# Two transformer layers on one core: the opening's stores reordered, preparation spread over more turns, first queries before the barrier, and the last batch's output in two halves

## The chip, the cores and the metric

One core of a Trainium2 chip. The metric is the device time of one execution in microseconds (us), as the median of several. The core's engines are PE (TensorE), DVE (VectorE), ACT (ScalarE), POOL (GpSimd) and SP (SyncE, which only issues DMAs here). Each runs its own queue of instructions in order, and they meet through semaphores. All matrix products and transposes write into PSUM. The kernel cuts it into three slots of 128 x 1024 float32 (`slot[0..2]`) that are used in turn (`RING = 3`), and `yspace`, two banks of 512 columns.

## The reference, cut to what matters

```python
x = L0_attn_x                                  # (4, 1024, 128) float32
xn = layernorm(x)
x = x + attn0(xn) + ffn0(xn)                   # 16 heads of 64, causal, keys and values from a latent of 128
                                               # ffn0: silu-gated, hidden 352, inputs and weights rounded to FP4 in blocks of 16
xn = layernorm(x)
x = x + attn1(xn) + ffn1(xn)                   # 16 heads of 8, bias by relative position, biases on q, k, v, out
return x                                       # ffn1: 512 wide, ternary weights, gelu
```

## The kernel before

It has three blocks, each with a barrier of all engines at its end (each engine drains its own work first).

**Block A, the opening.** SP and ACT issue the loads. The DVE takes mean and variance of each of the 32 tiles of 128 tokens (`first_moments(b)`, 8 tiles of a batch: 8 `bn_stats`, 8 `bn_aggr`), normalises batch 0 and rounds it to FP4 (`fp4`, ten steps, `fp4_steps` L1807), then rounds the two FFN weights. ACT takes the square roots (L353, L397). PE transposes by `groups`; ACT copies the results out of PSUM in the order of that list. The position biases of layer 1 are split in bfloat16 parts: `x_part` (parts 0, 1, 2, each the rest of the one before; DVE L310, L329; ACT L360). SP stores them to DRAM at L229 and L231 after `off_act` 8, and then sixteen rows-of-steps (`step_rows`, L236) after `steps_set` 4.

**Block B, layer 0.** 32 turns, one for each batch (4) and pair of heads (8). In a turn PE computes the scores of the pair (L745, in four passes of high and low halves of queries and keys), DVE takes row maxima (L1006, L1009), ACT the exponentials (L930), PE transposes the probabilities (L780) and multiplies by the values (L792). One tile of the FFN goes along (gates, `hidden`, `down`). At the end of a turn PE computes the next turn's queries (`next_queries`, L695), ACT copies them rounded (L892, the high half), and DVE subtracts to get the low half (L972), which frees the slot; meanwhile PE runs `down` (L832) and `project` (L841). DVE adds their results to `x_tok` (L1076, L1084). The first score tile of the next turn goes into the slot of the queries.

Batches 1 to 3 are prepared on the way, half a batch at a time (`PREPS = 6`, `PREP_TURNS = 2, 6, 10, 14, 18, 22`, counted from 0): DVE does eleven steps (`prep_ops`: normalise, L628, then the ten of `fp4_steps`) in the two turns before, at two places of each turn (`prep(it, 0)` ahead of L1076, `prep(it, 1)` behind L1084), cut as 1, 4, 3 and 3 steps. In the preparing turn PE transposes (L803) and makes the latent (L810), and ACT copies (L958). From turn 8 on, DVE also takes the layer 1 statistics of one finished tile in each turn (`moments_of`).

**Block D, layer 1.** Its opening projects queries, keys and values of each batch (list `CT`; L1417, L1425), with the FFN woven in (`up` L1434, `down` L1443), DVE normalising (L1716) and taking low halves (L1723). Then 16 quads (4 batches, 4 groups of four heads): per quad 32 tasks `x` (scores with bias, L1566 and L1572; exponential on ACT, L1661), 16 `attend` (L1538) and, except in the last quad, 32 tasks `m` for the maxima of the next quad (L1458, L1463; DVE L1678). `AV_BEFORE` and `M_BEFORE` are a hand-written order of these. The output of a batch is normalised in halves `c` of 512 tokens (`normalise`, L1769, L1771), gathered (`y_gather`, eight transposes, L1490), copied by ACT (`copy_yT`, L1652), projected (`project`, L1497), added (`add_out`, L1779) and stored. For the first three batches this lies inside the next quad (`YT_AT = 8`, `OUT_AT = 13`); for the last batch it comes after everything else (L1592 to L1595, store L1361).

## Time and profile before

| | |
|---|---|
| time, median of 3 runs | 2309.61 us (2309.35 to 2309.88) |
| the profiled execution's own time | 2304.86 us |
| its span, first to last instruction | 2303.1 us, granted TensorE clock 0.993 |
| block A (opening) | 0 to 50.8 us |
| block B (layer 0) | 50.8 to 1372.1 us |
| block D (layer 1) | 1372.1 us to the end; the quads from 1480.7 |
| busy | PE 2154.1 us (94%), PE weight loads 1347.6, DVE 1670.4 (73%), ACT 1319.2 (57%), POOL 47.5 |

A row of a timeline gives the start and the duration in us, the engine, the line of the kernel, the operation, what it writes and reads, how many instructions are merged (x), and in brackets how long the engine was idle before it and what released it. A `q` behind the engine's name is its instruction queue, which issues the DMAs.

### The profile page before, as it was taken

The page shows a single profiled execution, that of the slowest core. Times are in us where ns is not written, and L with a number is a line of the kernel's source. Part 1 is how long each engine was busy: PE and PEld are TensorE (multiplying, and loading weights), DVE is VectorE, ACT ScalarE, POOL GpSimd, SP SyncE. Part 2 cuts the span into 40 slices and gives each one's busy share as a digit, 9 for nine tenths or more (in the row PEclk, how much of TensorE's full clock was granted, in tenths as well). Part 3 has the DMA queues.
Part 4 walks back from the last instruction along what each step waited for, and adds up shares of the span by engine and source line. Part 5 has one row for each costly group of instructions (what it writes and reads, how often), then busy time and mean ns, then how long its engine had stood idle before and what let it go on. Part 6 is the DMA issues. An engine that isn't in the chain of part 4 may idle for free. (4 is left out here: it accounts for less than half of the span.)

```text
span 2303.1 us, 45467 instructions
## 1 busy us (share of the span) xinstructions
PE 2154.1 (94%) x19387; PEld 1347.6 (59%) x19387; DVE 1670.4 (73%) x2208; ACT 1319.2 (57%) x2121; POOL 47.5 (2%) x61
## 2 busy tenths in 40 slices
PE   3999999999999999999999999999999999999998
PEld 1666767666666676667667666544444444444443
DVE  6786777777777767777777775777777777777771
ACT  2655655546555465555655553366666666666666
POOL 3100000000000000000000000200000000000000
PEclk7999999999999999999999999999999999999999
DMA  5000000000000000000000019311011011111000
GB/s 121 1 1 1 1 1 1 1 1 1 1 1 1 1 1 1 1 1 1 1 1 1 1 20 223 69 20 20 20 20 29 23 29 33 23 20 20 11 2 11
DMA packets 41195, 42.60 MB, mean 18 GB/s; under 512 B 21345, under 2 KB 33601, under 8 KB 40866
## 3 DMA queue, kind: packets, MB, share of 16 engines
q1 hardware_dynamic: 39842, 39.05, 8.1%
q8 instruction: 154, 2.52, 0.5%
q10 hardware_dynamic: 1152, 0.64, 0.1%
q14 instruction: 47, 0.39, 0.1%
HBM read 27.71 MB, written 11.70 MB: 17 GB/s over the span
## 5 line engine op out<-in xcount | busy, mean ns | idle before, releaser
L1678 DVE TENSOR_REDUCE nm_half<-slot 128x2 f32<-128x1024 f32 x512 | 606.5, 1222 | 162.8 <-PE slot L1463 118.0
L1661 ACT ACTIVATE pT<-slot 128x1024 f32<-128x1024 f32 x512 | 505.8, 1026 | 269.0 <-PE slot L1572 214.5
L930 ACT ACTIVATE prob<-slot,negmax 128x1024 f32<-128x1024 f32 (+6 forms) x448 | 316.8, 718 | 265.3 <-DVE negmax L1009 192.0
L745 PE MATMUL slot<-k_hl,q_hl 64*128 64x512 f32 (+3 forms) x2560 | 355.8, 359 | 66.6 <-ACT prob L930 60.2
L745 PEld LDWEIGHTS slot<-k_hl,q_hl 64*128 64x128 f32 x2560 | 261.4, 186 | 106.6 <-ACT prob L930 79.8
L780 PEld LDWEIGHTS slot<-ident,prob 128*128 128x128 f32 x2304 | 254.1, 141 | 88.7 <-issue 61.4
L780 PE MATMUL slot<-ident,prob 128*128 128x128 f32 x2304 | 288.7, 275 | 0.9 <-DVE probT L609 0.9
L609 DVE COPY probT<-slot 128x768 f32<-128x768 f32 (+1 forms) x192 | 166.7, 868 | 152.0 <-PE slot L780 149.1
L792 PE MATMUL yspace<-probT,v_sb 128*64 128x512 f32 (+3 forms) x1536 | 276.2, 494 | 0.0
L1538 PE MATMUL yspace<-pT,v 128*32 128x512 f32 x2048 | 267.0, 604 | 1.6 <-ACT y_raw L1648 0.8
L1566 PE MATMUL slot<-qs,ks 49*128 49x512 f32 x1024 | 240.2, 471 | 15.1 <-DVE nm_half L1678 7.5
L911 ACT ACTIVATE probT<-slot 128x1024 f32<-128x1024 f32 x192 | 170.1, 886 | 146.4 <-PE slot L780 123.7
L1458 PE MATMUL slot<-ks,qs 48*128 48x512 f32 x1024 | 241.4, 471 | 11.0 <-DVE nm_half L1678 8.3
L1009 DVE TENSOR_REDUCE negmax<-slot 128x1 f32<-128x1024 f32 (+2 forms) x192 | 191.5, 1039 | 71.6 <-PE slot L768 71.6
L1458 PEld LDWEIGHTS slot<-ks,qs 48*128 48x128 f32 x1024 | 95.9, 184 | 152.7 <-DVE nm_half L1678 85.8
L1566 PEld LDWEIGHTS slot<-qs,ks 49*128 49x128 f32 x1024 | 95.5, 185 | 133.6 <-DVE nm_half L1678 59.3
L792 PEld LDWEIGHTS yspace<-probT,v_sb 128*64 128x64 f32 x1536 | 96.5, 136 | 113.0 <-issue 90.6
L1572 PE MATMUL slot<-band,flipb 64*128 64x176 bf16 (+4 forms) x3456 | 161.3, 226 | 0.0
L1572 PEld LDWEIGHTS slot<-band,flipb 64*128 64x128 bf16 x3456 | 106.2, 95 | 49.4 <-issue 36.4
L745 PE MATMUL yspace<-k_hl,q_hl 64*128 64x512 f32 (+2 forms) x512 | 110.4, 355 | 0.0
L1006 DVE TENSOR_REDUCE negmax<-slot 128x2 f32<-128x1024 f32 (+3 forms) x128 | 97.0, 800 | 0.0
L930 ACT ACTIVATION_READ_ACCUMULATOR prob<-slot,negmax 128x1 f32 x448 | 90.3, 202 | 0.0
(236 smaller groups left out, 2326.9 us busy)
## 6 DMA issues: line engine op xcount, KB each, us to landing
qs<-q_hi SPq DMA_DIRECT2D x64, 64.0 KB
qs<-q_lo SPq DMA_DIRECT2D x64, 64.0 KB
ks<-k_hi SPq DMA_DIRECT2D x64, 64.0 KB
ks<-k_lo SPq DMA_DIRECT2D x64, 64.0 KB
x_tok<-in_L_attn_x_dram SPq DMA_DIRECT2D x4, 512.0 KB, 7.0
q_hi<-qk_out SPq DMA_DIRECT2D x4, 512.0 KB, 4.1
q_lo<-qk_out SPq DMA_DIRECT2D x4, 512.0 KB, 5.7
k_hi<-qk_out SPq DMA_DIRECT2D x4, 512.0 KB, 6.0
```

Source lines behind the costliest of these rows:

```text
L745: nc.tensor.matmul(own_ps[a][:, o:o + m], q_hl[hq][own, i * P:(i + 1) * P], k_hl[hk][own, o:o + m], start=(k == 0), stop=(k == 3 and o + m ...
L780: last = nc.tensor.transpose(ps[:, a * BANK + j * P:a * BANK + (j + 1) * P], prob[a][:, p_at(4 * c + j, kt)], ident[:, :])
L792: last = nc.tensor.matmul(ybank[c][a * HS:(a + 1) * HS, j0:BANK], v_sb[:, kt, a * HS:(a + 1) * HS], probT[m % PT_BUFS][:, a, j0:BANK], sta ...
L911: copy_probT(act, it, m, lambda out, src: nc.scalar.activation(out, src, ACT.Copy))
L930: last = nc.scalar.activation(prob[a][:, p_at(i, 0, w)], ps[:, o:o + w], ACT.Exp, bias=negmax[:, i, a:a + 1], accum_out=sums[:, i, a:a + 1])
L1009: nc.vector.tensor_reduce(negmax[:, i, a:a + 1], ps[:, 0:w], AX.X, ALU.max, negate=True).then_inc(neg_ready, 1)
L1458: last_ = nc.tensor.matmul(ps[:, a * BANK:(a + 1) * BANK], qs[s][own, p, i * P:(i + 1) * P], ks[s][own, p, h * BANK:(h + 1) * BANK], start ...
L1538: last_ = nc.tensor.matmul(ymain[32 * j:32 * j + 32, :], v4[g % 2][:, kt, j, :], pT[j // 2][m % PT_DEEP][:, j % 2, :], start=(kt == 0), st ...
L1566: last_ = nc.tensor.matmul(ps[:, a * BANK:(a + 1) * BANK], ks[s][own, hp, kt * P:(kt + 1) * P], qs[s][own, hp, c * BANK:(c + 1) * BANK], s ...
L1572: last_ = nc.tensor.matmul(ps[:, a * BANK + o:a * BANK + o + w], flipb[own, f, :], band[own, f, 2 * g + hp, part, x:x + w], start=False, s ...
L1661: nc.scalar.activation(pT[hp][m % PT_DEEP][:, :, :], slot[at["x", n] % RING][:, :].rearrange("p (j t) -> p j t", t=BANK), ACT.Exp)\
L1678: nc.vector.tensor_reduce(nm_half[:, h, :, p * TPB + i], slot[pos % RING][:, :].rearrange("p (a t) -> p a t", t=BANK), AX.X, ALU.max, nega ...
```

## The change

Opening: SP issues the sixteen `step_rows` stores before the stores of `x_part`. ACT does a one-column square root early, and makes parts 1 and 2 of `x_part` at the groups `w2` and `gate` (before: `gate` and `down`). DVE makes the second rest (L329) before it rounds the FFN weights. Only batch 1's statistics stay in the opening; those of batches 2 and 3 are taken in turns 6 and 7 of block B, with their square root on ACT in turn 8 and their reciprocal on DVE.

Block B: preparing turns 3, 6, 11, 14, 18, 21, with DVE's steps in three turns, six places, cut as 1, 1, 4, 2, 2 and 1. The first score tile waits for fewer things, in another order. At the end PE computes queries and keys of batch 0 of layer 1 into slots 0 and 1 before the barrier; block D then finds them there.

Block D: in the last quad the first four tiles of the last batch are gathered behind task 23 and projected behind task 26, with copy, addition and store following; the other four at the end.

```diff
@@ opening, SP
+                    sp.wait_ge(steps_set, 4)
+                    for j in range(TPB):
+                        for r in range(2):
+                            o = T - j * P
+                            sp.dma_start(step_rows[:, TPB * r + j, :], steps_sb[:, r, o:o + T].bitcast(F32)).then_inc(steps_saved, 16)
                     sp.wait_ge(off_act, 8)
...
-                    sp.wait_ge(steps_set, 4)
...
@@ opening, DVE
+                    dve.wait_ge(off_act, 7)
+                    nc.vector.tensor_tensor(rest[:, :, :], rest[:, :, :], x_part[:, :, 1, :], ALU.subtract).then_inc(rest_step, 1)
+
                     dve.wait_ge(grp_full, group_at["xq", 0, 1] + 1)
...
-                    for b in range(1, B):
-                        first_moments(b)
+                    first_moments(1)
                     dve.wait_ge(std0_done, 2)
-                    nc.vector.reciprocal(rstd0[:, TPB:TILES], std0[:, TPB:TILES]).then_inc(r0_set, 1)
+                    nc.vector.reciprocal(rstd0[:, TPB:2 * TPB], std0[:, TPB:2 * TPB]).then_inc(r0_set, 1)
@@ opening, ACT
                     act.wait_ge(pool_ready, 3)
+                    nc.scalar.activation(absum[:, 0:1], eps_col[:, 0:1], ACT.Sqrt)
                     act.wait_ge(m0_step, 2)
...
-                        if kind in ("gate", "down"):
-                            part = 1 if kind == "gate" else 2
+                        if kind in ("w2", "gate"):
+                            part = 1 if kind == "w2" else 2
@@ block B
-                PREP_TURNS = [4 * j + 2 for j in range(PREPS)]
+                PREP_TURNS = [3, 6, 11, 14, 18, 21]
+                MOMENT_TURNS, ROOT_TURN = (6, 7), 8
...
+                def late_inverse(dve):
+
+                    dve.wait_ge(std0_done, 3)
+                    nc.vector.reciprocal(rstd0[:, 2 * TPB:TILES], std0[:, 2 * TPB:TILES]).then_inc(r0_set, 1)
+                    dve.wait_ge(r0_set, 3)
...
-                            if n == 0:
-
-                                pe.wait_ge(hi_done, 2 * it + 2)
-                                freed(pe, it - 1, TK)
...
+                            elif n == 0:
+
+                                freed(pe, it - 1, TK)
+                                assert at["s0"] % RING == TQ % RING
+                                own_ps[1] = score_claim(1)[:, 0:w]
+                                own_ps[0] = score_claim(0)[:, 0:w]
...
-                                if n == 0 and k == 2:
-
-                                    freed(pe, it - 1, TQ)
...
+                    freed(pe, TURNS - 1, TQ)
+                    for m, s in enumerate((0, 1)):
+                        if s:
+                            freed(pe, TURNS - 1, TDN)
+                        for h in range(2):
+                            nc.tensor.matmul(slot[s][:, h * BANK:(h + 1) * BANK], w4T[:, m, :], xnT[:, h * BANK:(h + 1) * BANK], start=True, stop=True)
...
+                        if it == ROOT_TURN:
+                            late = slice(2 * TPB, TILES)
+                            act.wait_ge(m0_step, 4 + 8)
+                            nc.scalar.activation(std0[:, late], moments0[:, late, 1], ACT.Sqrt, bias=eps_col[:, 0:1]).then_inc(std0_done, 1)
...
-                            if it in (turn - 2, turn - 1):
-                                first, last = ((0, 1), (1, 5), (5, 8), (8, PREP_OPS))[2 * (it - turn + 2) + place]
+                            if turn - 3 <= it < turn:
+                                first, last = ((0, 1), (1, 2), (2, 6), (6, 8), (8, 10), (10, PREP_OPS))[2 * (it - turn + 3) + place]
...
+                        if it in MOMENT_TURNS:
+                            late_moments(2 * MOMENT_TURNS.index(it) + place)
+
+                    def late_moments(n):
+
+                        t0 = 2 * TPB + 4 * n
+                        dve.wait_ge(m0_step, 4 + 2 * n)
+                        for k in range(4):
+                            op = nc.vector.bn_stats(sixes4[:, k, :], x_tok[:, t0 + k, :])
...
@@ block D
+                LAST_YT, LAST_OUT = T0_AT + 2, T0_AT + 5
...
+                        if n == LAST_YT and last:
+                            tasks.append(("yT", 0))
+                        if n == LAST_OUT and last:
+                            tasks.append(("out", 0))
+                    return tasks + ([("yT", 1), ("out", 1)] if last else [])
...
-                        if b:
-                            ring_freed(pe, 0, c_at["T", b])
+                        if b == 0:
+
+                            assert pos % RING == "QK".index(kind)
+                            pe.nop().then_inc(full1[pos % RING], 1)
+                            return
...
+                            if last and n == LAST_YT:
+                                pe.wait_ge(misc_free, y0_use(z) + 1)
+                                y_gather(r, at["yT", 0], range(4))
+                            if last and n == LAST_OUT:
+                                project(r, at["yT", 0], at["out", 0], range(4))
...
-                            y_gather(r, at["yT"])
-                            project(r, at["yT"], at["out"])
+                            y_gather(r, at["yT", 1], range(4, TPB))
+                            project(r, at["yT", 1], at["out", 1], range(4, TPB))
```

ACT's copy, DVE's addition and SP's store of the last batch are cut in the same two halves.

## Rows read from the trace of the kernel before

**Rows 1.** the page: PE's busy tenths in 40 equal slices of the span
```profile
PE   3999999999999999999999999999999999999998
```

**Rows 2.** the opening's timeline: start us, us, engine, line, operation [idle before]
```profile
7.78 1.28 ACT L353 ACT_TABLE_LOAD   x1 [7.78 <-DVE moments L297]
...
9.07 0.30 ACT L353 ACTIVATE std<-moments,eps_col 128x8 f32<-128x8 f32 x1
...
24.56 1.40 DVE L321 TENSOR_SCALAR steps_sb<-ones,dcol 16x1024 fp32r<-16x1024 f32 x2
...
40.35 1.61 DVE L293 BATCH_NORM_STATS2 sixes<-x_tok 128x6 f32<-128x128 f32 x8
...
45.22 0.30 DVE L338 RECIPROCAL rstd<-std 128x24 f32<-128x24 f32 x1 [0.38 <-ACT std L397]
...
50.80 2.00 POOL L645 TENSOR_SCALAR xn_early<-W1T,tinv 128x512 f32<-128x512 f32 x1 [35.46 <-SPq L450]
```

**Rows 3.** the timeline of SP's queue in the opening
```profile
35.71 0.77 SPq L229 DMA_DIRECT2D x_vals<-x_part  x1
...
38.54 8.90 SPq L236 DMA_DIRECT2D step_rows<-steps_sb  x16
```

**Rows 4.** the timeline of the joint of turns 1 and 2
```profile
138.76 0.29 DVE L1076 TENSOR_TENSOR x_tok<-slot,x_tok 128x128 f32<-128x128 f32 x1 [0.36 <-PE slot L832]
...
139.15 1.22 DVE L972 TENSOR_TENSOR q_hl<-slot,q_hl 128x1024 fp32r<-128x1024 f32 x1
...
140.54 1.23 DVE L1084 TENSOR_TENSOR x_tok<-slot,x_tok 128x1024 f32<-128x1024 f32 x1 [0.17 <-PE slot L841]
...
140.60 1.71 PEld L745 LDWEIGHTS slot<-k_hl,q_hl 64*128 64x128 f32 x16 [0.28 <-issue]
```

**Rows 5.** the timeline: the same addition in turns 0, 2 and 3
```profile
99.92 1.22 DVE L1084 TENSOR_TENSOR x_tok<-slot,x_tok 128x1024 f32<-128x1024 f32 x1 [0.18 <-PE slot L841]
...
183.64 1.22 DVE L1084 TENSOR_TENSOR x_tok<-slot,x_tok 128x1024 f32<-128x1024 f32 x1 [0.18 <-PE slot L841]
...
224.09 1.23 DVE L1084 TENSOR_TENSOR x_tok<-slot,x_tok 128x1024 f32<-128x1024 f32 x1 [0.18 <-PE slot L841]
```

**Rows 6.** the timeline around preparing turn 2: DVE's maximum, PE's added work
```profile
143.74 2.35 DVE L1009 TENSOR_REDUCE negmax<-slot 128x1 f32<-128x1024 f32 x2
...
175.86 0.60 PE L803 MATMUL slot<-ident,xn_half 128*128 128x128 f32 x4
...
178.30 1.12 PE L810 MATMUL slot<-xnT,wkd 128*128 128x512 f32 x2
```

**Rows 7.** the timeline of ACT at the end of turn 8
```profile
426.76 1.02 ACT L892 ACTIVATE q_hl<-slot 128x1024 fp32r<-128x1024 f32 x1 [2.81 <-PE slot L695]
```

**Rows 8.** the timeline of the first microseconds of block D
```profile
1372.53 2.14 DVE L1716 TENSOR_SCALAR xn_tok<-x_tok,moments,rstd 128x128 f32<-128x128 f32 x8 [0.41 <-PEq L450]
...
1373.04 3.67 PE L1417 MATMUL slot<-xnT,w4T 128*128 128x512 f32 x8 [2.18 <-DVEq L1673]
...
1376.82 2.57 DVE L1723 SCALAR_TENSOR_TENSOR qk_out<-slot,bqk,qk_out 128x1024 fp32r<-128x1024 f32 x2
...
1377.76 0.29 ACT L1603 ACTIVATE std<-moments,eps_col 128x8 f32<-128x8 f32 x1
```

**Rows 9.** window, length, busy us (count) of PE, PEld, DVE, ACT, POOL
```profile
2278.30:2288.30 10.00, 10.00 (x146) 4.94 (x140) 0.00 (x0) 7.54 (x9) 0.00 (x0) 1.00 0.01 2
```

**Rows 10.** the timeline of the end
```profile
2293.81 1.09 PE L1490 MATMUL slot<-ident,y_tok 128*128 128x128 f32 x8 [0.67 <-DVE y_tok L1771]
...
2294.94 1.02 ACT L1652 ACTIVATE y_T<-slot 128x1024 f32<-128x1024 f32 x1 [2.52 <-PE slot L1490]
...
2296.02 2.05 PE L1497 MATMUL slot<-w4T,y_T 128*128 128x128 f32 x16 [1.11 <-ACT y_T L1652]
...
2298.18 1.22 DVE L1779 TENSOR_TENSOR x_tok<-slot,x_tok 128x1024 f32<-128x1024 f32 x1 [4.42 <-PE slot L1497]
...
2299.43 0.41 SPq L1361 DMA_DIRECT2D out_dram<-x_tok  x1
```

More of the change, by code:

```diff
@@ L231, in _ @@
                         sp.dma_start(m_vals.ap()[diag].rearrange("a h n -> h a n"), m_part[:, diag, :]).then_inc(bias_out, 16)
-                    sp.wait_ge(steps_set, 4)
-                    for j in range(TPB):
-                        for r in range(2):
-                            o = T - j * P
-                            sp.dma_start(step_rows[:, TPB * r + j, :], steps_sb[:, r, o:o + T].bitcast(F32)).then_inc(steps_saved, 16)
                     sp.wait_ge(hot_saved, 32)
@@ L517, in two_layers @@
                 PREPS = 2 * (B - 1)
-                PREP_TURNS = [4 * j + 2 for j in range(PREPS)]
+                PREP_TURNS = [3, 6, 11, 14, 18, 21]
+                MOMENT_TURNS, ROOT_TURN = (6, 7), 8
                 PREP_AT = TQ
-                assert PREP_TURNS[-1] < (B - 1) * PAIRS and PREP_AT % RING == 0
+                assert len(PREP_TURNS) == PREPS and all(t <= (j // 2 + 1) * PAIRS - 2 for j, t in enumerate(PREP_TURNS)) and PREP_AT % RING == 0
                 def lap(it, n):
@@ L1648, in copy_y, with copy_yT @@
                             nc.scalar.activation(y_raw[c][:, :], ymain[:, :], ACT.Copy).then_inc(y_copied, 1)
-                        def copy_yT():
-                            ring_filled(act, r, at["yT"])
-                            nc.scalar.activation(y_T[:, :], slot[at["yT"] % RING][:, :], ACT.Copy).then_inc(free1[at["yT"] % RING], 1)
+                        def copy_yT(task="yT", cols=slice(0, T)):
+                            ring_filled(act, r, at[task])
+                            nc.scalar.activation(y_T[:, cols], slot[at[task] % RING][:, cols], ACT.Copy).then_inc(free1[at[task] % RING], 1)
                         for n in range(XT):
@@ L1664, in one @@
                                 copy_yT()
+                            if n == LAST_YT and last:
+                                copy_yT(("yT", 0), slice(0, BANK))
                         copy_y(1)
                         if last:
-                            copy_yT()
+                            copy_yT(("yT", 1), slice(BANK, T))
                     quads(act, one)
@@ L1796, in one @@
                                 nm_out(z + 1)
+                            if last and n == LAST_OUT:
+                                add_out(b, ("out", 0), 0, 4)
                         if last:
                             normalise(z, g, 1, Y1_END)
-                            add_out(b)
+                            add_out(b, ("out", 1), 4, TPB)
                     quads(dve, one)
```

54 lines of the change are left out of this document (32 added, 22 removed).

## The prediction

> **What bounds the kernel now.** I read the slices of the page first: TensorE is at nine tenths or more in 38 of 40 slices [rows 1]. Only the first slice and the tail have air in them, so a large gain must come from the opening, from the last microseconds, or from the joints of the turns where TensorE briefly waits. Then I read the timeline of the opening. The DVE is the busy engine and makes its last value at 45.22 us; the second block begins at 50.80 us [rows 2]. Between the two only SP works: its sixteen stores of step_rows are issued from 38.54 on, for 8.90 us, behind four stores that start at 35.71 [rows 3]. So SP ends the opening, and the DVE is 5 us behind it. Third, the joint of two turns of the middle stage: TensorE's first score load comes at 140.60, and what it waits for is the low half of the next queries, which the DVE ends at 139.15 + 1.22 = 140.37 [rows 4]. I looked at all 32 joints: 0.23 us between those two in 29, 0.26 in three. Last, the end: a chain of single steps, each engine waiting for the one before it [rows 10].
>
> **Opening.** (a) The sixteen stores need only the step rows, ready at 24.56 + 1.40 = 25.96 us [rows 2]. They are moved ahead of the four stores that wait for a later value. SP's queue then runs 25.96 + 8.90 + 2.83 (35.71 to 38.54) = 37.7, and with the 3.36 us that lie between its last issue (47.44) and the next block, the block could begin at 41.1. (b) The table load that ACT makes at 7.78 us, with the DVE waiting behind it, is drawn to before the wait by a one-column root: 1.29 us off the DVE's chain and off (a), so 39.8 for SP. The activation behind the load starts at 9.07, with it done. By the Trainium skill (ScalarE: Activation LUTs, What ACT_TABLE_LOAD costs) a switch also costs a drain of about 1.38 us; here the row shows no such gap; with it the gain would be 2.7 us. (c) The statistics of two of four batches leave the opening: 40.35 to 45.22, less the 0.38 us wait for the root, is 4.49 us [rows 2]. The small subtraction L329 only changes places with the quantisation (0), and ACT's copy of its result is then long done. DVE's end: 45.52 - 1.29 - 4.49 = 39.7, plus 0.4 to 0.9 for the barrier (0.41 at the other joint of blocks, where the DVE waited for it [rows 8]) gives 40.6. SP at 39.8 and DVE at 40.6 are near each other; the DVE is last. Saving: 50.80 - 40.6 = **10.2 us**, bounds 8.2 (SP's landings come 2 us later behind twenty stores in a row) and 11.2.
>
> **Joint of two turns.** The old order waits on four things before the first score; the new one on three, with the slot of the low half last. After a single wait TensorE follows in 0.06 us (y_T ends at 2294.94 + 1.02 = 2295.96, L1497 starts at 2296.02 [rows 10]); with four it takes 0.23 [rows 4]. One wait less lies between: bounds 0 and 0.17 a turn. I take 0.11, since two waits still stand before the load. TensorE's own project work ends just before (its load idles only 0.28 us), so there is nothing behind to hide it. 32 x 0.11 = **3.5 us** (0 to 5.6). The wait between the second and third pass goes too; its condition is the same release that the first claim already had, so 0.
>
> **Preparation.** Ends of turns lie 40.62 us apart before a preparing turn (99.92 to 140.54), 43.10 with it (to 183.64), 40.45 after it (to 224.09) [rows 4, 5]. The six turns alike, but one which has 0.8 more; there the clock was at half for 3.4 us, which I leave as noise. Of the 2.65 us, TensorE's own work is two groups of transposes like L803 (0.60 each) and the latent product L810, which holds the array 0.97 of its 1.12 us [rows 6]; with their waits I count 1.85. The rest, 0.8, has a cause on the DVE: after the add L1084 (ends 141.77) it runs three steps of preparation, and so takes up the first maximum only at 143.74 [rows 4, 6]. The score was ready near 142.8, about 2.2 us after the first load. So about 1.0 us of DVE time is free there. The new split puts there 0.68, 0.9 and 0.69 us instead of 1.4 and 2.1: all fit, so the 0.17 and the 0.8 go: 6 x 0.97 = 5.8 us. Ahead of the queries' low half the DVE has the time to 138.76, where it waits for L832; the old pieces there take 1.6 us and leave it 0.36 idle [rows 4]. The new ones take 1.45 us at most, 1.9 with the statistics of later turns: hidden, barely. The late statistics add four pieces of 4.49 / 4 = 1.12 us in turns 6 and 7; the two behind the add overrun the free 1.0 by about 0.15 each, 0.3 together. Net **5.5 us** (0 to 6.3). The late root: ACT waits 2.81 us in turn 8 before the copy of the queries [rows 7]; a load and a root, 1.28 + 0.30 [rows 2], fit, and the reload for the exponentials falls in ACT's wait of the next turn. Cost 0; without cover 1.3. By the same page's drain the load and root would take 2.97 us and overrun by 0.2.
>
> **First queries and keys early.** TensorE ends the middle stage at 1373.04 - 2.18 = 1370.86 and would now go on for 3.67 us [rows 8], to 1374.5. Every engine waits at the barrier for TensorE. Before, the DVE came last (1372.53 less its wait of 0.41: 1372.12) and began the last stage at 1372.53; now it begins at about 1374.8, **2.3 us later**, and so does SP. What was late next in the last stage is not the product: the DVE normalises and takes statistics until 1376.82, before it touches the first low half; ACT's root, which waits for them, ran at 1377.76, because ACT was still copying keys [rows 8]. The copies of queries and keys now start with the block, so ACT has 0.94 us of slack. The turned batch, the table load, the first gelu and the second "up" product hang on that root: 2.3 - 0.9 = **1.4 us lost** here (bounds: 0.8 gained, if the barrier did not wait; 2.3 lost). From there TensorE is dense and carries it to the end.
>
> **The end.** Half of each step leaves the tail [rows 10]: gather 1.09 us, half is 0.5; y_T 1.02, 0.4; project 2.05, 1.0; add 1.22, 0.5; the store, which takes from 2299.43 to the span's end at 2303.1, between 0 and half of its 3.6 us: I take 0.8, since landing is mostly not size. Together 3.2. (By the Trainium skill, DMA: Bandwidth & Descriptors, Anatomy of one DMA, a transfer costs 2.0 us and its bytes over 436 GB/s, fitted for another queue; half of 512 KB would save 0.6.) The moved halves, 0.5 + 1.0 us, go to TensorE at 2278 to 2288, where it is busy 10.00 of 10.00 us [rows 9], so they are paid there; ACT's half copy fits its idle time (7.54 of 10 busy). The ring has three slots; by my walk through it no claim is late. Net **1.7 us** (0.2 to 2.6).
>
> **Sum.** 10.2 + 3.5 + 5.5 - 1.4 + 1.7 = 19.5 us. The profiled execution (2304.9, span 2303.1) would come to 2285.4. The median of the three timed runs, 2309.6, is 4.7 above it, for reasons the trace doesn't hold; the same difference gives **2290.1 us**.
>
> **Rivals.** *Early queries pay* (0.12): the barrier lets TensorE's queue drain beside it. For: the products need no one else. Against: nothing in the trace; no engine enters the last stage before the DVE's last add has ended. +0.8 instead of -1.4: 2287.9. *Preparation is TensorE's own* (0.10): the 2.65 us stay however the DVE's pieces lie. For: transposes and product cover most of it. Against: the 0.17 in a turn that adds no TensorE work at all. 2295.6. *Opening half gained* (0.06): SP's 5 us go, but the DVE isn't shorter, as it waits for ACT's reordered copies. 50.80 - 45.9 = 4.9 instead of 10.2: 2295.4. *Slower* (0.02): the DVE's pieces ahead of the low half overrun their 1.9 us. Then the queries are late in all 18 turns that carry one; from (19.5 + 4.6) / 18 = 1.3 us each the kernel is slower by over 0.2%. At 1.5 us each: 19.5 - 27 gives 2317.1. Against: the same DVE steps have rows, and sum to less.
>
> **How the numbers follow.** The forecast has 0.70. Its own range, from the bounds above, not all at one end: 2285 to 2295. The range reaches to the rivals at 2295.6: 2284.5 to 2297. 0.2% of the time, 4.6 us, is about what a measurement of this kernel can tell from no change. All cases but the last are below 2305: faster 0.97, same 0.01, slower 0.02.
>
> **What would show it.** The second block starts near 40.6 us with the DVE last. First score load 0.10 to 0.15 us after the low half. Preparing turns 42.2 us, the turns before them as the rest (40.35). The last stage's DVE starts 2.3 us later against the last add, its root 1.4. ACT's last exponential 1.5 us later in its quad, the tail after it 3.2 shorter. Wrong would be: SP's landing above 41 us, the joint still at 0.23, the first maximum still late in preparing turns.

## The result, and the profile after

The changed kernel takes **2287.53 us** (median of four runs, 2285.36 to 2288.07), against 2309.48 us before (four runs, 2309.28 to 2309.88): a ratio of 0.9903 (95% interval 0.9886 to 0.9920), 22.0 us less. Forecast were 2290.1 us and a range of 2284.5 to 2297.0, so the range holds it. The profiled execution of the changed kernel took 2287.97 us (span 2286.2); that of before took 2304.86 (span 2303.1). So the two traces differ by only 16.9 us, where the prediction's steps summed to 19.5. Both differences need an account: what is missing in the trace, and what the timed runs gained beyond it.

| stage, from the two profiles | before | after | gained | forecast |
|---|---|---|---|---|
| start to the big addition of turn 0 | 99.92 | 93.11 | 6.8 | 10.2 |
| that addition to the one of turn 31 | 1270.98 | 1260.56 | 10.4 | 9.0 (3.5 + 5.5) |
| last big addition to ACT's first exponential | 109.85 | 111.17 | -1.3 | -1.4 |
| the 15 quads before the last, first exponential to first exponential | 773.7 | 773.8 | -0.1 | 0 |
| last quad, first to last exponential | 35.08 | 37.22 | -2.1 | -1.5 |
| tail, from the start of the last exponential | 13.54 | 10.32 | 3.2 | 3.2 |

The page's PE slices of the changed kernel show the same picture as [rows 1], a long nine-tenths with air at both ends.

The opening of the changed kernel, its timeline (start us, us, engine, line, operation, idle before and its releaser):
```profile
4.78 1.28 ACT L352 ACT_TABLE_LOAD   x1 [4.78 <-issue]
...
7.68 0.30 ACT L354 ACTIVATE std<-moments,eps_col 128x8 f32<-128x8 f32 x1 [1.40 <-DVE moments L297]
...
8.25 5.49 DVE L304 TENSOR_SCALAR xn_tok<-x_tok,moments,rstd 128x128 f32<-128x128 f32 x8
...
25.76 8.73 SPq L231 DMA_DIRECT2D step_rows<-steps_sb  x16
...
34.52 0.77 SPq L234 DMA_DIRECT2D x_vals<-x_part  x1
...
40.59 0.20 DVE L338 RECIPROCAL rstd<-std 128x8 f32<-128x8 f32 x1 [0.37 <-ACT std L398]
...
42.41 3.75 PE L690 MATMUL slot<-latT,wkv_all 128*128 128x512 f32 x4 [3.40 <-ACTq L905]
...
51.20 3.65 PE L752 MATMUL slot<-k_hl,q_hl 64*128 64x512 f32 x16 [2.46 <-DVEq L999]
```
Against [rows 2, 3]: the table load is made at 4.78, before its statistics are there; SP's sixteen stores start at 25.76 and not at 38.54; and the DVE's last value (40.59) has only 8 elements a partition and not 24. Two rows are not as forecast: L304 with 5.49 us, and the first scores (51.20) with 3.65 us, and both come up again below.

The joint of turns 1 and 2, and the big addition of the first turns (the one of preparing turn 3 is the last row):
```profile
93.11 1.22 DVE L1120 TENSOR_TENSOR x_tok<-slot,x_tok 128x1024 f32<-128x1024 f32 x1 [0.17 <-PE slot L851]
...
132.06 1.22 DVE L994 TENSOR_TENSOR q_hl<-slot,q_hl 128x1024 fp32r<-128x1024 f32 x1
...
133.40 1.72 PEld L752 LDWEIGHTS slot<-k_hl,q_hl 64*128 64x128 f32 x16 [0.17 <-issue]
...
133.46 1.23 DVE L1120 TENSOR_TENSOR x_tok<-slot,x_tok 128x1024 f32<-128x1024 f32 x1 [0.17 <-PE slot L851]
...
173.82 1.22 DVE L1120 TENSOR_TENSOR x_tok<-slot,x_tok 128x1024 f32<-128x1024 f32 x1 [0.17 <-PE slot L851]
...
176.03 2.36 DVE L1045 TENSOR_REDUCE negmax<-slot 128x1 f32<-128x1024 f32 x2 [0.38 <-PE slot L778]
...
215.94 1.23 DVE L1120 TENSOR_TENSOR x_tok<-slot,x_tok 128x1024 f32<-128x1024 f32 x1 [0.17 <-PE slot L851]
```
Between the end of the low half (132.06 + 1.22 = 133.28) and the first score load (133.40) lie 0.12 us, where [rows 4] have 0.23. The additions are 40.35 and 40.36 us apart and then, over a preparing turn, 42.12, where [rows 4, 5] give 43.10. The first maximum behind a preparing addition (176.03, 2.21 us after it) now waits 0.38 for TensorE's score; in [rows 6] it came 3.20 us after its addition (143.74 against 140.54) with no wait of its own.

The handover to the last stage, to be held against [rows 8]:
```profile
1353.47 3.60 PE L900 MATMUL slot<-xnT,w4T 128*128 128x512 f32 x8
...
1353.67 1.22 DVE L1120 TENSOR_TENSOR x_tok<-slot,x_tok 128x1024 f32<-128x1024 f32 x1 [1.42 <-PE slot L851]
...
1357.46 2.14 DVE L1771 TENSOR_SCALAR xn_tok<-x_tok,moments,rstd 128x128 f32<-128x128 f32 x8 [2.56 <-PEq L451]
...
1361.87 0.30 ACT L1656 ACTIVATE std<-moments,eps_col 128x8 f32<-128x8 f32 x1 [1.65 <-DVE moments L1761]
```
The DVE's addition ends at 1354.89 and it starts the next block 2.56 us later and not 0.41, released by TensorE's queue, whose 3.60 us of added products end at 1357.07.

The last quad and the end, against [rows 9, 10]:
```profile
2262.88 0.63 PE L1538 MATMUL slot<-ident,y_tok 128*128 128x128 f32 x4 [0.28 <-ACT pT L1714]
...
2269.12 1.16 PE L1545 MATMUL slot<-w4T,y_T 128*128 128x128 f32 x8
...
2280.15 0.66 PE L1538 MATMUL slot<-ident,y_tok 128*128 128x128 f32 x4 [0.68 <-DVE y_tok L1826]
...
2282.76 0.69 DVE L1834 TENSOR_TENSOR x_tok<-slot,x_tok 128x512 f32<-128x512 f32 x1 [2.67 <-PE slot L1545]
...
2283.48 0.38 SPq L1404 DMA_DIRECT2D out_dram<-x_tok  x1
```
The steps of the tail are about half as long as in [rows 10]; the first half's gather and product (2262.88, 2269.12) stand inside the quad.

### The profile page after: what moved, and what is told of

Its sections match the earlier page's. It is cut to its first block and busy times, and to the rows that moved or that the text cites. A ratio compares the mean times of both kernels' runs of the same rounds, so it can differ in the third digit from the quotient of the medians.

```text
span 2286.2 us, 45447 instructions
## 1 busy us (share of the span) xinstructions
PE 2154.7 (94%) x19387; PEld 1343.7 (59%) x19387; DVE 1672.4 (73%) x2210; ACT 1322.8 (58%) x2126; POOL 47.6 (2%) x61
```

## The experiments

All are the changed kernel with one part undone or one suspect added, except the first and the tenth, which start from the kernel before. "First addition" is the start of the big addition of turn 0, "sum of the turns" runs from there to the big addition of turn 31.

**1. Before, once more** (no edit).

> The kernel before, once more, to see how steady its profile is and where the 4.7 us lie by which its timed runs stand above its first profiled execution. Theory clock: the timed runs hold more stretches at half TensorE clock than the profiled one (which had one of 3.4 us, worth 0.8 us); then this profile shows more such stretches, or a time near 2304.9 when it has none. Rival: the timed runs have something the profile doesn't show; then this profile has the same turns (40.46 us, 43.1 with preparation) and again a span near 2303. Either way the joints stay at 0.23 us and block B starts near 50.8 us.

Measured: 2309.89 us (ten runs, 2305.84 to 2313.06) beside 2309.94 (thirteen); ratio 1.0001 (0.9992 to 1.0011). Profiled it took 2305.84 (span 2304.0), joints 0.23, turns as before. The timed runs lie nearly in the order of their granted clock: 2305.7 to 2308.2 at 0.992, 2307.5 to 2310.0 at 0.991, 2309.8 to 2313.1 at 0.990, 2314.39 at 0.988. The profile has one stretch in the middle of the kernel in which TensorE is busy throughout and yet has half its clock, 1.2 GHz; the row of the 7 us before it stands above it (window, length, then busy us and count of PE, PEld, DVE, ACT, POOL, the granted clock, DMA share, GB/s):
```profile
594.50:601.50 7.00, 5.74 (x56) 4.45 (x56) 6.90 (x10) 3.44 (x7) 0.00 (x0) 1.00 0.01 2
601.50:604.90 3.40, 3.40 (x23) 3.12 (x25) 1.21 (x2) 2.26 (x6) 0.00 (x0) 0.51 0.00 0
```
In the row ahead of it TensorE is idle for 1.26 of the 7 us. The first profile of before had its own stretch, elsewhere:
```profile
478.00:481.40 3.40, 3.40 (x26) 3.01 (x23) 1.40 (x3) 1.99 (x6) 0.00 (x0) 0.50 0.02 5
```
So the 4 to 5 us between the profiles and the medians of before are not noise: the median run had a lower clock than the profiled one. The changed kernel's timed runs are granted 0.993 to 0.995 and lie at its profile's time.

**2. No early queries and keys.**
```diff
-                    freed(pe, TURNS - 1, TQ)
-                    for m, s in enumerate((0, 1)):
...
-                        if b == 0:
...
-                            pe.nop().then_inc(full1[pos % RING], 1)
-                            return
```

> The changed kernel, with the first queries and keys of layer 1 computed after the barrier again. My theory: computing them before it costs 1.3 us, so this one is 1.3 us faster than the changed kernel; from the last big addition of block B to the first exponential of the quads 109.9 us instead of 111.2, and the DVE's first instruction of block D 0.4 us behind that addition's end instead of 2.6. Rival, early products pay: 0.8 us slower than the changed kernel, 112.0 us. The rest of the trace unchanged.

Measured: 2285.69 us (2284.53 to 2287.16), ratio 0.9898 (0.9881 to 0.9914), 1.8 less than the changed kernel. Last big addition to first exponential: 109.89, with 111.17 in the changed kernel and 109.85 before. The timeline of the handover:
```profile
1352.67 1.23 DVE L1113 TENSOR_TENSOR x_tok<-slot,x_tok 128x1024 f32<-128x1024 f32 x1 [1.43 <-PE slot L851]
...
1354.31 2.14 DVE L1760 TENSOR_SCALAR xn_tok<-x_tok,moments,rstd 128x128 f32<-128x128 f32 x8 [0.41 <-PEq L451]
```
The DVE is back at 0.41 behind its addition. The early products cost 1.3 us: shown by these rows. The times of the two kernels overlap; the verdict rests on the rows.

**3. No halves** (gather, projection, addition and store of the last batch whole again, at the end).
```diff
-                        if n == LAST_YT and last:
-                            tasks.append(("yT", 0))
-                        if n == LAST_OUT and last:
-                            tasks.append(("out", 0))
-                    return tasks + ([("yT", 1), ("out", 1)] if last else [])
+                    return tasks + (["yT", "out"] if last else [])
```

> The changed kernel with the last batch's output in one piece at the end again. From the two profiles the halves take 3.2 us off the tail and put 2.1 us into the last quad, so this one should be 1.1 us slower: the stretch from the last quad's first to its last exponential 35.1 us instead of 37.2, the tail behind it 13.5 instead of 10.3. Rival: part of the 2.1 us in the quad has another cause (the clock or the rows before it); then the stretch stays above 35.1.

Measured: 2288.33 us (2286.87 to 2289.17), ratio 0.9908 (0.9891 to 0.9925). Last quad 35.08, tail 13.53, as before to 0.01. With the halves 37.22 and 10.32, so they gain 1.1 us net.

**4. The old joint.**
```diff
+                            if n == 0:
+                                pe.wait_ge(hi_done, 2 * it + 2)
+                                freed(pe, it - 1, TK)
...
-                            elif n == 0:
...
+                                if n == 0 and k == 2:
+                                    freed(pe, it - 1, TQ)
```

> The changed kernel with the four waits of before at the first score tile. Theory, the waits' number sets the joint: 0.23 us again between the low half's end and the first score load, turns 40.46 instead of 40.35, 31 turns x 0.11 = 3.4 us slower. Rival, the joint was shortened by where the DVE's pieces lie: the joint stays at 0.12 us and nothing is lost.

Measured: 2288.99 us (2288.22 to 2290.88), ratio 0.9913 (0.9896 to 0.9930). The joint of turns 1 and 2:
```profile
131.54 1.23 DVE L995 TENSOR_TENSOR q_hl<-slot,q_hl 128x1024 fp32r<-128x1024 f32 x1
...
132.99 1.72 PEld L756 LDWEIGHTS slot<-k_hl,q_hl 64*128 64x128 f32 x16 [0.28 <-issue]
```
132.99 - 132.77 = 0.22 again, and the 0.28 of idle load as in [rows 4]; turns of 40.47, preparing ones 42.23, sum of the turns 1263.9 and not 1260.6. The joint is worth 3.3 us. The edit brings back both the fourth wait and the old order of the waits, so which of the two costs the 0.11 us a turn was not separated.

**5. The old order of the stores.**
```diff
-                    sp.wait_ge(steps_set, 4)
-                    for j in range(TPB):
...
                     sp.wait_ge(off_act, 8)
...
+                    sp.wait_ge(steps_set, 4)
+                    for j in range(TPB):
```

> The changed kernel with the order of SP's stores of before: the four stores of the bias parts first, then the sixteen of step_rows. In the changed kernel SP was ready at 38.7 us and the DVE at 41.0. Theory, the DVE ends the opening and the stores' order is worth only the overhang: SP waits for the parts until 27.5 us, issues four and sixteen stores (2.8 + 8.9 us), to 39.2, and 3.4 us behind them block B begins near 42.6 instead of 41.2, so 1.4 us slower than the changed kernel. Rival, the order itself is the gain: block B begins near 50 us.

Measured: 2287.66 us (2286.49 to 2289.20), ratio 0.9912 (0.9898 to 0.9927). The timeline of SP and of the next block:
```profile
27.65 0.77 SPq L229 DMA_DIRECT2D x_vals<-x_part  x1
...
30.49 8.86 SPq L236 DMA_DIRECT2D step_rows<-steps_sb  x16
...
42.61 2.00 POOL L656 TENSOR_SCALAR xn_early<-W1T,tinv 128x512 f32<-128x512 f32 x1 [27.05 <-SPq L451]
```
TensorE starts the second block at 43.67, 1.26 us later than in the changed kernel (42.41). So, with the rest of the change in place, the order of SP's stores is worth 1.3 us by this pair of profiles; the medians (2287.66 and 2287.53) do not show it. The four stores that had started at 35.71 [rows 3] start at 27.65 although SP's program is the old one: what they wait for now comes earlier from ACT, and that, not the place of the stores, took most of SP's delay away.

**6. No early table load.**
```diff
-                    nc.scalar.activation(absum[:, 0:1], eps_col[:, 0:1], ACT.Sqrt)
```

> The changed kernel without the early one-column root. In the changed kernel the DVE's normalisation of batch 0 started 1.4 us earlier than before but took 5.5 us instead of 4.6. Theory, POOL: the DVE's fast copies wait while POOL works on the same memory side, and POOL is busy until about 12.5 us whatever the DVE does, so an earlier start is mostly waited away. Then without the early root the normalisation takes 4.6 us again and the DVE's last value comes only 0.3 to 0.5 us later (41.1 to 41.3 instead of 40.8). Rival, the 5.5 us come from elsewhere (loads landing): then the DVE's end is 1.3 us later, 42.1.

Measured: 2286.48 us (2285.15 to 2288.34), ratio 0.9907 (0.9893 to 0.9922). The timeline:
```profile
7.80 1.28 ACT L353 ACT_TABLE_LOAD   x1 [7.80 <-DVE moments L297]
...
9.67 4.64 DVE L304 TENSOR_SCALAR xn_tok<-x_tok,moments,rstd 128x128 f32<-128x128 f32 x8
...
40.93 0.20 DVE L338 RECIPROCAL rstd<-std 128x8 f32<-128x8 f32 x1 [0.37 <-ACT std L397]
```
The load is back on the DVE's chain, the normalisation starts 1.42 us later (9.67 against 8.25), and yet the last value is ready only 0.34 us later (40.93 against 40.59), since the eight steps now take 4.64 and not 5.49 us. Taken as they stand, three quarters of what the early load saves are lost again in the steps behind it. But one profile each is thin for this. Nine profiles of kernels with the opening of the changed kernel or with only SP's stores reordered (the changed one, experiments 2 to 5, 8, 9, 11, 12) have 4.54 to 5.56 us for the eight steps and 39.40 to 40.73 for the start of the last value. This experiment's 4.64 lies inside the one and its 40.93 is 0.2 beyond the other, so what the early load is worth is not settled.

**7. POOL held back until the DVE has normalised.**
```diff
                     pool.wait_ge(fold_set, 6)
+                    pool.wait_ge(xn0_set, 1)
                     nc.gpsimd.memset(ones[:, :], 1.0).then_inc(flip_step, 1)
```

> The changed kernel with one wait added: POOL holds its work on ones, flip, hot rows, step rows and query weights until batch 0 is normalised. Theory POOL: the eight normalising steps take 2.1 us as in block D, not 5.5, and the opening's DVE chain ends up to 3.4 us earlier, less what the held POOL work (about 10 us) takes from the DVE's fast steps later; I expect block B 1.5 to 3 us earlier. Rival: the steps still take 0.6 us each, and nothing is gained or SP's and TensorE's use of POOL's results comes late and block B starts later.

Measured: 2286.56 us (2284.97 to 2287.47), ratio 0.9906 (0.9892 to 0.9921). The timeline:
```profile
8.20 2.14 DVE L305 TENSOR_SCALAR xn_tok<-x_tok,moments,rstd 128x128 f32<-128x128 f32 x8
...
14.36 3.10 POOL L277 TENSOR_SCALAR_AFFINE_SELECT hot<-hot 16x1024 f32<-16x1024 f32 x2
...
18.57 1.94 DVE L1879 TENSOR_TENSOR tmp_s<-tmp_s,tmp_e 128x1024 f32<-128x1024 f32 x1
...
19.33 3.81 POOL L284 TENSOR_SCALAR wq_all<-wq_all 128x1024 f32<-128x1024 f32 x1
...
40.32 0.20 DVE L339 RECIPROCAL rstd<-std 128x8 f32<-128x8 f32 x1 [0.37 <-ACT std L399]
```
The normalisation takes 2.14 us without POOL beside it, just what the same eight steps take in [rows 8]; in the changed kernel it is 5.49. That POOL's work is what stretched it is thus shown. But the gain moved on: POOL's steps now lie beside other steps of the DVE, and these stretch instead. In the changed kernel the DVE step of L1879 above has this row, 1.22 us and not 1.94:
```profile
20.27 1.22 DVE L1878 TENSOR_TENSOR tmp_s<-tmp_s,tmp_e 128x1024 f32<-128x1024 f32 x1
```
Four such steps of the DVE are 0.7 to 0.8 us longer each. Its last value comes 0.27 us earlier, and not the 3.35 that the one group saves; that is less than kernels with one and the same opening differ by (experiment 6). POOL and TensorE start the second block at 41.08 and 42.15, 0.26 us earlier than in the changed kernel. The expectation of 1.5 to 3 us is missed.

**8. The old preparation turns** (the statistics of the later batches stay in turns 6 and 7).
```diff
-                PREP_TURNS = [3, 6, 11, 14, 18, 21]
+                PREP_TURNS = [4 * j + 2 for j in range(PREPS)]
...
-                            if turn - 3 <= it < turn:
-                                first, last = ((0, 1), (1, 2), (2, 6), (6, 8), (8, 10), (10, PREP_OPS))[...]
+                            if it in (turn - 2, turn - 1):
+                                first, last = ((0, 1), (1, 5), (5, 8), (8, PREP_OPS))[...]
```

> The changed kernel with the preparation's turns and its cut into four places of before. Theory: the DVE pieces behind the addition delay the first maximum; turns before a preparing one become 0.17 us longer, preparing turns 0.9 us longer (42.1 to 43.0): 6 x 1.05 = 6.3 us slower. Rival, the turns' excess was TensorE's own: preparing turns stay at 42.1.

Measured: 2299.08 us (five runs, 2294.48 to 2299.13, clocks 0.990 to 0.992), ratio 0.9953 (0.9939 to 0.9967): 11.5 slower than the changed kernel. The big additions of turns 0 to 2:
```profile
90.42 1.22 DVE L1120 TENSOR_TENSOR x_tok<-slot,x_tok 128x1024 f32<-128x1024 f32 x1 [0.17 <-PE slot L851]
...
131.04 1.22 DVE L1120 TENSOR_TENSOR x_tok<-slot,x_tok 128x1024 f32<-128x1024 f32 x1 [0.17 <-PE slot L851]
...
174.13 1.23 DVE L1120 TENSOR_TENSOR x_tok<-slot,x_tok 128x1024 f32<-128x1024 f32 x1 [0.17 <-PE slot L851]
```
40.62 and 43.09: the old figures, although the joints are the new ones, so the turns before a preparing one lost 0.27 and the preparing ones 0.98. Six times 1.25 is 7.5. The rest goes with the clock. Four stretches between opening and end lie in this profile at half of it, the longest the second row here (in the 7 us ahead of it TensorE is idle for 1.70):
```profile
461.70:468.70 7.00, 5.30 (x53) 4.21 (x54) 6.92 (x8) 2.54 (x5) 0.00 (x0) 1.00 0.00 0
468.70:478.90 10.20, 10.10 (x51) 7.96 (x50) 5.06 (x6) 7.47 (x18) 0.00 (x0) 0.50 0.01 2
```
The three turns that hold the first three take 41.27, 41.43 and 46.59 us where their like take 40.45, 40.63 and 43.10: 5.1 more. With the 7.5 that is the whole growth of the sum of the turns (1273.25 for 1260.56).

**9. No early queries and keys, the first half of the end one place later.**
```diff
-                LAST_YT, LAST_OUT = T0_AT + 2, T0_AT + 5
+                LAST_YT, LAST_OUT = T0_AT + 3, T0_AT + 6
```
and the edit of experiment 2.

> The changed kernel without the early queries and keys, and with the first half of the last batch gathered behind task 24 and projected behind task 27 of the last quad (23 and 26 before). Theory: in the changed kernel the gather waited for a slot of the ring (0.28 us idle, and the tasks behind it stood), which took 0.6 of the 2.1 us that the quad grew; one task later the slot is free: last quad 36.6 us instead of 37.2, tail unchanged at 10.3, so 0.6 us faster than without the early products alone and 1.9 faster than the changed kernel. Rival: the growth is TensorE's work alone and the quad stays at 37.2.

Measured: 2285.18 us (2285.05 to 2286.72) beside 2310.05, ratio 0.9893 (0.9878 to 0.9908). The last quad takes 36.74 and not 37.22; the first half's gather has no wait ahead of it:
```profile
2263.14 0.66 PE L1527 MATMUL slot<-ident,y_tok 128*128 128x128 f32 x4
```
The tail, expected unchanged at 10.3, takes 10.83 in this profile, because TensorE's last products fall at half clock there (from 2280.2; they take 1.67 us and not 1.16). Experiment 11, whose end is that of the changed kernel, has 10.82 by a stretch at the same distance. Leaving that aside, the rows make this version 1.3 + 0.5 = 1.8 us better than the changed kernel, and its median is 2.4 lower. Its median is the lowest of all that ran; the times of the two overlap, and in the one profile the quad's 0.5 is lost again in the tail, so the worth of the later place is shown for the quad only.

**10. The new preparation on the kernel before** (the edit of experiment 8 the other way round, nothing else).

> The kernel before with only the preparation's new turns and its new cut into six places. In turns alone it should give 6 x 1.05 = 6.3 us (preparing turns 42.2, turns before them 40.46). Theory, late maxima starve TensorE and the clock falls: the timed runs of before show granted clocks of 0.990 to 0.992, those of the changed kernel 0.993 to 0.995; then this kernel's timed runs show 0.993 or more and the gain in timed runs is 10 to 11 us, more than the 6.3. Rival, the clock differs for another part of the change (the opening): then clocks stay at 0.990 to 0.992 and the gain is 6.3.

Measured: 2300.93 us (2298.05 to 2301.80) beside 2310.05, ratio 0.9956 (0.9939 to 0.9972). The additions of turns 1 to 3:
```profile
141.18 1.23 DVE L1084 TENSOR_TENSOR x_tok<-slot,x_tok 128x1024 f32<-128x1024 f32 x1 [0.17 <-PE slot L841]
...
181.63 1.23 DVE L1084 TENSOR_TENSOR x_tok<-slot,x_tok 128x1024 f32<-128x1024 f32 x1 [0.17 <-PE slot L841]
...
223.87 1.22 DVE L1084 TENSOR_TENSOR x_tok<-slot,x_tok 128x1024 f32<-128x1024 f32 x1 [0.17 <-PE slot L841]
```
40.45 and then 42.24 over the preparing turn; before, the turn ahead of a preparing one took 40.62 and the preparing one 43.10, so 1.03 a pair are gained, 6.2 in six. The timed gain is 9.1, and the granted clock of the timed runs is 0.992 to 0.993 beside 0.990. That lies between the two cases expected (6.3, and 10 to 11). The 2.9 us above the turns' gain go with the clock; that is part of the 4.7, not all of it.

**11. Late maxima without the rest**: eight statistics of no use behind the addition of turns 23 to 30, which carry no preparation.
```diff
+                        if 23 <= it < 31 and place == 1:
+                            for _ in range(2):
...
+                                for k in range(4):
+                                    op = nc.vector.bn_stats(junk4[:, k, :], x_tok[:, k, :])
```

> The changed kernel with useless work of the DVE (eight more statistics, 1.65 us) behind the big addition in each of turns 23 to 30. About 1.1 us of DVE time is free there, so the first maximum comes 0.6 us late and the eight turns behind grow by 0.4 to 0.6 us each (40.35 to 40.8 or 40.95). Clock theory: some of these turns also get a stretch at half clock 7 to 8 us behind the addition, so the granted clock of the timed runs falls to 0.992 or less and the time rises by more than the 3 to 5 us of the delays. Rival: the clock stays at 0.993 to 0.995 and the time rises by the delays alone.

Measured: 2292.15 us (2290.79 to 2293.60), ratio 0.9922 (0.9907 to 0.9937), 4.6 more than the changed kernel. Two additions, one of the eight turns between them:
```profile
1031.62 1.22 DVE L1133 TENSOR_TENSOR x_tok<-slot,x_tok 128x1024 f32<-128x1024 f32 x1 [0.17 <-PE slot L853]
...
1072.58 1.23 DVE L1133 TENSOR_TENSOR x_tok<-slot,x_tok 128x1024 f32<-128x1024 f32 x1 [0.17 <-PE slot L853]
```
40.96 and not 40.35 in seven of the eight, and the last, which is shorter in every kernel, takes 39.88 and not 39.27: 0.61 more each, 4.9 in all, which is the whole timed loss. No half-clock stretch fell into these turns, and the timed runs have clocks of 0.992 to 0.996. The first maximum comes 2.83 us after the start of the big addition and not 2.20.

**12. The same eight statistics, four at each place of the turn.**
```diff
+                        if 23 <= it < 31 and True:
+                            for _ in range(1):
...
+                                for k in range(4):
+                                    op = nc.vector.bn_stats(junk4[:, k, :], x_tok[:, k, :])
```

> The same useless work as in the kernel with late maxima, but four statistics ahead of the queries' low half and four behind the addition, in the same turns. Both pieces (0.83 us) fit the DVE's free time, so turns stay at 40.35 us, the granted clock at 0.993 to 0.995 and the time at that of the changed kernel. Rival, DVE work as such costs: the turns grow as in the other kernel.

Measured: 2285.60 us (2284.29 to 2285.73), ratio 0.9892 (0.9877 to 0.9907). The same turns take 40.35:
```profile
1028.09 1.22 DVE L1133 TENSOR_TENSOR x_tok<-slot,x_tok 128x1024 f32<-128x1024 f32 x1 [0.17 <-PE slot L853]
...
1068.44 1.23 DVE L1133 TENSOR_TENSOR x_tok<-slot,x_tok 128x1024 f32<-128x1024 f32 x1 [0.17 <-PE slot L853]
```
So the same DVE work costs 4.9 us in one place and nothing in the other: it is the place against the free time that counts, not the amount. This kernel's span, 2282.2, is also 4.0 below that of the changed one, with the same opening in the program. The windows of the two over the same 3.6 us, the changed kernel first:
```profile
51.10:54.70 3.60, 3.50 (x18) 2.72 (x19) 0.00 (x0) 0.00 (x0) 3.52 (x3) 0.53 0.02 5
```
```profile
51.10:54.70 3.60, 2.89 (x30) 2.22 (x27) 3.54 (x4) 2.29 (x5) 3.44 (x3) 1.00 0.00 0
```
At full clock the scores are done and the DVE and ACT already work on them; at half clock TensorE is still at them. The first addition comes at 89.30 and not at 93.11. Of these 3.8 us, 1.2 lie ahead of the second block, which POOL starts at 40.17 here and at 41.34 there.

## Why the prediction was right, point by point

**Bound.** TensorE bounds the kernel as said: in the 15 quads before the last it is busy 748.4 of 773.7 us before and 748.5 of 773.8 after.

**Opening: right that the stores and the DVE end it, 3.4 us too much in the profile.** 6.8 us were gained, 10.2 forecast, below the lower bound of 8.2. Two terms failed. First, (b) counted all of the 1.29 us of the table load as gained by the DVE. The normalisation did begin 1.39 us earlier (8.25 for 9.64), the load and nothing behind it, but it grew from 4.55 us to 5.49, so 0.94 came back. Experiment 7 shows that POOL's work beside it stretches it. The DVE's last value moved by 4.73 us (45.52 to 40.79), not 5.8, and the second block by 9.5 (50.80 to 41.34). Other kernels with the same opening start that block at 40.17 (experiment 12), 40.27 (3) and 40.45 (4), so the 40.6 that was forecast lies inside what this opening gives from one execution to the next.

Second, behind the barrier I let the time to the first addition stand, and there the clock took 2.7 us. The opening's own half clock runs 5.33 us beyond TensorE's first product (42.41) in the changed kernel, and 2.86 before (51.88 to 54.74), so the first scores begin 1.13 us later against that product (the changed kernel first, columns as in experiment 1):
```profile
42.41:47.74 5.33, 5.33 (x7) 2.23 (x8) 0.48 (x1) 1.02 (x1) 5.17 (x4) 0.50 0.00 2
51.88:54.74 2.86, 2.86 (x4) 1.30 (x5) 0.00 (x0) 0.00 (x0) 2.86 (x2) 0.50 0.01 3
```
Then the first scores fell into a stretch of their own at half clock (51.16 to 54.57) and took 3.48 us to the first fold and not 1.91. Four kernels without that second stretch have their first addition at 89.30 (experiment 12), 90.42 (8), 90.86 (2) and 90.78 (7), a gain of 9.1 to 10.6, in which the forecast lies. Six others with it (experiments 3 to 6, 9 and 11) have 91.46 to 94.33. That it comes in some profiles and not in others of one and the same opening is shown; what decides it is not.

That "SP ends the opening" [rows 3] was right, but experiment 5 shows the cause one step further back: SP stood behind ACT, and reordering SP's stores is worth 1.3 us once ACT is early. My sum gave the 5 us between SP and the DVE to the order of the stores. What the order and ACT's earlier parts each do without the other was not run. The rival "opening half gained" (a start at 45.9) is excluded by the start at 41.34.

**Joint: right.** 0.23 to 0.12 us in all 32, 0.11 as taken between the bounds; experiment 4 gives 3.3 of the 3.5, the turns' sum holding 31 joints. The upper bound of 5.6 should read 5.4 (32 x 0.17). The reason given, one wait fewer, stands beside the new order of the waits, and no run separates them.

**Preparation: right in each turn, and its worth beyond the turn missed.** Preparing turns 42.11 (42.2 said), those before them 40.35 (as said), late statistics 0.1 each (0.15 said), root 0 (0 said). The prediction's 1.85 us for TensorE's own work in a preparing turn does not follow from the terms beside it, which add up to 2.17 (0.60 + 0.60 + 0.97) before any wait; measured are 1.77 (42.12 less 40.35), so the figure was good and its derivation was not. The sum of the turns fell by 10.4, 9.0 forecast; 0.8 of the difference is the stretch at 478.0 of the profile of before, and a preparing turn with the one ahead of it gained 1.03 (experiment 10) and not 0.97. The rival "preparation is TensorE's own" is excluded by experiments 8 and 10; of "slower" nothing is seen, since no turn with preparation grew. Experiments 11 and 12 show the mechanism by itself: DVE work that fits the time before its first maximum is free, and what overruns delays the turn.

**Early queries: right.** -1.3 measured, -1.4 said, and the DVE waits for TensorE's queue at the block's end, so the rival that they pay is excluded (experiment 2). The prediction's slack of 0.94 us for ACT was nearly right as well: the DVE began 2.15 us later behind its addition, of which 1.3 arrived, so 0.83 were absorbed.

**End: sign right, size a little high.** The tail gives 3.2 as said; the quad lost 2.1 and not 1.5. Of this 0.3 is the gather's wait (row 2262.88) for its slot of the ring, which my walk through the ring had called never late; one place on (experiment 9) the wait is gone and the quad is 0.5 shorter. The store's part of the tail was 0.8 by the forecast and 0.9 by the rows (issue to end of the span 2.69 us and not 3.63). Net 1.1, and 1.7 was forecast.

**The offset: the step that failed most, and it hid the others.** "The same difference gives 2290.1" took the 4.7 us between profile and median of before as the same for both kernels, and left a turn that was 0.8 us longer at half clock as noise. The 4.7 go with that kernel's clock (experiment 1). For the changed kernel the profile (2287.97) and the median (2287.53) agree. So the steps gave 2.6 us less in the trace than said (16.9 for 19.5), and the vanished offset gave 5.1 more (22.0 for 16.9). The two errors have opposite signs, and 2.6 us are left between forecast and result. So the steps were right in kind, and that the total lies this near is partly luck. With either error alone the time would still have been inside the range (2292.7 or 2285.0).

**What remains open.** The clock part goes with the old preparation turns: putting them back makes the kernel 11.5 us slower where the turns account for 7.5 (experiment 8), and the new ones alone on the kernel before gain 9.1 where the turns give 6.2 (experiment 10). The stretches in the middle of the runs that were looked at (478.0, 601.5, 384.1, 345.8, 427.7, 468.7, all inside block B) all begin 7.0 to 8.1 us behind the big addition of a turn with added DVE work behind it. Four more lie in the first microseconds of block D (1357.1 in experiment 7, 1369.8 in 8, 1367.0 in 10, 1364.9 in 11), with no such turn just ahead. My theory was that late maxima leave TensorE idle there and that its clock falls for it. Experiment 11 made late maxima alone, in eight turns, and got no stretch: in this form the theory is not confirmed. It is not refuted either. In the three profiles with the old preparation (before, experiments 1 and 8) 38 turns have added DVE work behind their addition and five got a stretch; at that rate eight turns show none about one time in three (an estimate from these counts). What else of the old split brings them, such as where it lies against the first TensorE work of preparation, was not separated.

## What to carry to other kernels

Work put on an engine beside the critical one is free up to a gap that can be read in the trace (here 1.0 us before the first maximum) and costs its whole overrun behind it: split it over the gaps, and test a place with useless work of the same length before building on it. A difference between the profile's time and the median has to be explained, by the granted clock of the timed runs, before it is carried over to the changed kernel. Where two queues end a stage, ask of the later one what it waited for before giving its delay to the order of its own instructions.

## What the runs showed of the hardware that I had not expected

**POOL slows the DVE by far more than a little.** Eight DVE steps of 128x128 take 2.14 us alone and 5.49 beside POOL's work (experiment 7); between kernels with the same opening they took 4.54 to 5.56, by how the steps fell against POOL's, and in the changed kernel's trace most of their late ends come 0.1 us behind the end of an instruction of POOL. Steps of the DVE with two inputs of 128x1024 took 1.94 to 1.99 us beside POOL's select and scale, and 1.23 alone or beside POOL's memsets (13.06 in experiment 7). The Trainium skill (GPSIMD Engine Reference, Specifications) has POOL's way to SBUF shared with the DVE and names contention with DVE steps that have two inputs in SBUF or run in a mode that takes both ports. The traces agree for the two-input steps (1.94 for 1.23); of the eight normalisation steps, with one tensor input, no row shows the mode.

**Half clock in a kernel that is 94% busy.** TensorE is 94% busy over the span, and yet stretches of 3.4 us and once 10.2 at 1.2 GHz come in single turns; a short one costs its turn 0.8 to 1.0 us, the long one 3.5, and the half clock at the start of the second block 2.7 more than before (1.13 + 1.57). TensorE is busy throughout the stretches, but not ahead of them (5.74 and 5.30 of 7.00 us in the rows of experiments 1 and 8). The changed kernel and that of experiment 8 do the same work in another order; the granted clocks of their timed runs are 0.993 to 0.995 and 0.990 to 0.992, which goes with the 4 us by which their times differ beyond their turns.

**The waits ahead of an instruction have a price of their own.** With the four old waits ahead of the first load 0.23 us pass after the low half is ready, with the three new ones in their new order 0.12: 3.3 us over 31 joints. Behind the single wait of another instruction it is 0.06 [rows 10]. That the number of waits makes the difference, and not their order, is not shown.
